# Moving the front half of a circuit layer out of the stage between attention and experts and into the attention loop

## The reference, cut to what matters

```python
x = x + cross_attention(layernorm(x), ctx, ctx)      # 32 batches, 64 queries, 1601 keys, 16 heads of 16
# the circuit layer, on y = layernorm(x):
c  = cumprod(cos(y), over the 16 columns of a head)
x1 = layernorm(y + c) * gamma1 + beta1
q  = cumprod(cos(x1[..., :16]))
f  = relu(q @ w1.T + b1) @ w2.T + b2                  # 16 -> 1024 -> 256
x  = x + layernorm(x1 + f) * gamma2 + beta2
x  = x + experts(layernorm(x))                        # shared expert + top 2 of 7
```

## Time and profile before

| what | value |
|---|---|
| time, median of 3 runs | 1946.18 us (1945.27 to 1947.3) |
| profiled execution, first to last instruction (span) | 1941.7 us |
| attention, from the first batch to the start of the last | 58 to 1388 us |
| last batch and its last weighing | 1388 to 1434 us |
| circuit layer to the first load of the experts | 1434 to 1537 us |
| experts | 1537 to 1941.7 us |

### The profile page before, as it was taken

The page is one execution under the profiler, slowest core; times in us unless marked ns, Lnnn a source line. Parts: engine busy times, 40 slices in busy tenths (PEclk is TensorE's granted clock), DMA queues, the critical chain, the costliest instruction groups (busy, mean ns, idle before and its releaser), DMA issues. The chain is left out here.

```text
span 1941.7 us, 46658 instructions
## 1 busy us (share of the span) xinstructions
PE 1876.6 (97%) x18832; PEld 1777.8 (92%) x18832; DVE 1468.1 (76%) x2796; ACT 1136.1 (59%) x1921; POOL 652.9 (34%) x643
## 2 busy tenths in 40 slices
PE   7899999999999999999999999999879889999998
PEld 5899999999999999999999999999867789999998
DVE  6777778777777777777777778777788567766667
ACT  2465666666566656666665566656765436665552
POOL 3222223322222323222223232223031126888860
PEclk9899999999999999999999999999989799999999
DMA  8666666666666666666666666667510236666633
GB/s 272 170 155 162 156 174 169 164 157 159 161 153 167 170 167 167 157 158 157 159 167 164 170 165 162 156 163 189 149 60 23 76 118 209 225 220 218 229 115 132
DMA packets 146790, 313.85 MB, mean 162 GB/s; under 512 B 57888, under 2 KB 77216, under 8 KB 143120
## 3 DMA queue, kind: packets, MB, share of 16 engines
q1 hardware_dynamic: 140672, 295.03, 56.2%
q0 software_dynamic: 4752, 13.38, 2.3%
q10 hardware_dynamic: 1152, 2.47, 0.5%
HBM read 134.20 MB, written 18.35 MB: 79 GB/s over the span
## 5 line engine op out<-in xcount | busy, mean ns | idle before, releaser
L453 ACT COPY a_pT<-a_pst 128x512 f32<-128x512 f32 x768 | 421.2, 583 | 409.0 <-PE a_pst L963 409.0
L459 ACT ACTIVATE a_probs<-a_probs,a_nmax 128x1601 f32<-128x1601 f32 x256 | 418.8, 1636 | 140.0 <-DVE a_probs L636 139.8
L636 DVE TENSOR_SCALAR_CACHE_REDUCE a_probs<-a_pss 128x1608 f32<-128x1608 f32 x256 | 467.3, 1825 | 12.8 <-PE a_pss L952 12.3
L963 PE MATMUL a_pst<-a_id,a_probs 128*128 128x128 f32 (+1 forms) x3328 | 452.6, 275 | 13.7 <-ACT a_pT L453 11.5
L963 PEld LDWEIGHTS a_pst<-a_id,a_probs 128*128 128x128 f32 (+1 forms) x3328 | 382.8, 141 | 51.1 <-issue 21.0
L355 POOL TENSOR_TENSOR a_tick<-a_tick 128x1 f32<-128x1 f32 x62 | 12.0, 193 | 953.4 <-DMA a_raw<-in_ctxT 892.1
L654 DVE TENSOR_SCALAR a_khi<-a_psk,a_bk 128x402 fp32r<-128x402 f32 x250 | 158.5, 634 | 142.9 <-PE a_psk L917 141.3
L360 POOL TENSOR_TENSOR a_clo<-a_raw,a_chi 128x402 fp32r<-128x402 f32 x240 | 247.0, 1060 | 4.8
L952 PE MATMUL a_pss<-a_kst,a_bd 96*128 96x402 f32 x1024 | 240.7, 357 | 6.4 <-DVE a_v L661 5.6
L915 PE MATMUL a_pso<-a_whi,a_chi 128*128 128x256 f32 (+1 forms) x806 | 241.9, 300 | 0.0
L917 PE MATMUL a_pso<-a_whi,a_clo 128*128 128x256 f32 (+1 forms) x806 | 227.2, 282 | 0.0
(11 more groups left out here) (251 smaller groups left out, 3511.7 us busy)
## 6 DMA issues: line engine op xcount, KB each, us to landing
a_kst<-a_khi SPq DMA_DIRECT2D x1008, 100.5 KB, 2.6
a_kst<-a_klo SPq DMA_DIRECT2D x504, 100.5 KB, 2.6
a_raw<-in_ctxT SPq DMA_DIRECT2D x60, 804.0 KB, 5.5
f_gur<-in_wgu SPq DMA_DIRECT2D x24, 1408.0 KB, 6.2
f_dr<-in_wd SPq DMA_DIRECT2D x24, 768.0 KB, 7.2
a_bd<-q_scr SPq DMA_DIRECT2D x192, 32.0 KB, 2.0
e_big<-ys_scr SPq DMA_DIRECT2D x8, 512.0 KB, 6.7
a_pT<-in_ctxT SPq DMA_DIRECT2D x2, 1608.0 KB, 9.3
```

What stands on the lines that cost most here:

```text
L453: nc.scalar.copy(pT[:, p % HALF, 4 * i:4 * i + 4, :], ps_t[:, i % 2, :].rearrange("p (t q) -> p t q", q=P)).then_inc(t_copied_act, 1)
L459: nc.scalar.activation(pr, pr, ACT.Exp, bias=nmax[:, b, p:p + 1], scale=-1.0, accum_out=esum[:, b, p:p + 1]).then_inc(probs_ready, 1)
L636: nc.vector.tensor_scalar(probs[:, p % 2, :].rearrange("p (b k) -> p b k", b=QK), ps_s[:, :, 0:KQ], -SCALE, None, ALU.mult, ALU.min, accum ...
L963: mm = nc.tensor.transpose(ps_t[0:r, i % 2, (t % 4) * P:(t % 4 + 1) * P], probs[:, p % 2, t * P:t * P + r], a_id_sb[:])
```

## The change

The front half of the circuit layer is done for each row tile inside the attention loop. For tile `it - 1`, in the batch with b = 0 and behind the two context splits, GpSimd takes the norm's power, the angle in turns, and the cosine as a polynomial (`row_cosines`, `cosines`: 18 instructions, of which 14 are 128x256). In the batch with b = 1, DVE makes the running product, the sum and the row statistics (`cumulate`, four instructions, behind the last copy of p = 2), and GpSimd centres the rows (`centre_rows`). SP stores them to a new scratch `a_scr`. Tile 15 goes the same way after attention. ACT's angles, sines and centring 1 are gone, and DVE's rounding. The second cosine is done by GpSimd for tiles 0 to 14 in one piece (`q_cosines(0)`) in the last batch and for tile 15 alone later. Groups are now five ((0,4), (4,4), (8,4), (12,2), (14,2)), the order lists are new, `idle_work` is gone, and contraction is ordered row tile by row tile.

The context is split in place: `raw` lies where `c_lo` lies, with room for both halves, so SP issues both loads together.

```diff
+            def cosines(width):
+
+                u, r, w, g = (z[:, 0:width] for z in (turn, left, square, cosine))
+                v(nc.gpsimd.tensor_scalar(w, u, ROUND, None, ALU.add))
+                v(nc.gpsimd.tensor_scalar(w, w, ROUND, None, ALU.subtract))
+                v(nc.gpsimd.tensor_tensor(out=r, in0=u, in1=w, op=ALU.subtract))
+                v(nc.gpsimd.tensor_tensor(out=w, in0=r, in1=r, op=ALU.mult))
+                v(nc.gpsimd.tensor_scalar(g, w, HALF_SINE[4], HALF_SINE[3], ALU.mult, ALU.add))
+                for k in (2, 1, 0):
+                    v(nc.gpsimd.tensor_tensor(out=g, in0=g, in1=w, op=ALU.mult))
+                    v(nc.gpsimd.tensor_scalar(g, g, HALF_SINE[k], None, ALU.add))
+                v(nc.gpsimd.tensor_tensor(out=g, in0=g, in1=g, op=ALU.mult))
+                v(nc.gpsimd.tensor_tensor(out=g, in0=g, in1=w, op=ALU.mult))
+                v(nc.gpsimd.tensor_scalar(g, g, -2.0, 1.0, ALU.mult, ALU.add))
+                v(nc.gpsimd.tensor_copy(by_head(heads[:, 0:width])[:, :, 0], by_head(g)[:, :, 0]))
+                nc.gpsimd.memset(by_head(g)[:, :, 0], 0.0).then_inc(cos_ready, 1)
...
+            def batches(it, first, last):
                 for b in range(2):
                     n = 2 * it + b
...
+                    if b == 0 and not first:
+                        row_cosines(it - 1)
...
+                    if b == 1 and not first:
+                        centre_rows(it - 1)
...
+            def cumulate(i):
+
+                dve.wait_ge(cos_ready, i + 1 if i < NT - 1 else NT + 1)
+                nc.vector.tensor_tensor_scan(left[:], cosine[:], heads[:], 0.0, ALU.mult, ALU.add).then_inc(scanned, 1)
+                dve.wait_ge(scanned, 3 * i + 1)
+                nc.vector.scalar_tensor_tensor(out=square[:], in0=turn[:], scalar=2.0 * np.pi, in1=left[:], op0=ALU.mult, op1=ALU.add).then_inc(scanned, 1)
+                dve.wait_ge(scanned, 3 * i + 2)
+                nc.vector.bn_stats(out=row_stats[:], in_=square[:]).then_inc(scanned, 1)
+                dve.wait_ge(scanned, 3 * i + 3)
+                nc.vector.bn_aggr(out=x1_mv2[:, i, :], in_=row_stats[:]).then_inc(cumulated, 1)
...
-                        if n == B - 1 and p in TURNS_IN:
...
-                                round_turns(i)
-                                leave_turns(i)
+                        if b == 1 and p == 2 and not first:
+                            cumulate(it - 1)
...
-            "turn_last.0 turn_end.0 weigh.0 project.0 turn_q.0 expand.0 expand.1 expand.2 expand.3 expand.4 expand.5 expand.6 expand.7 contract.0 turn_q.1 expand.8 "
...
+            "turn_q.0 turn_last.0 expand.0 expand.1 turn_end.0 expand.2 expand.3 weigh.0 expand.4 expand.5 expand.6 expand.7 project.0 turn_q.1 contract.0 expand.8 "
```

More of the change, by code:

```diff
@@ L300, in batches @@
                     if not last:
-                        if not (first and b == 0):
-                            sp.wait_ge(ctx_split, NC * (n + 1))
-                        load_ctx(n + 2, 0)
+                        sp.wait_ge(kv_filled, STEPS * (n + 1))
+                        for k in range(NC):
+                            load_ctx(n + 2, k)
+                    if b == 0 and it > 1:
+                        sp.wait_ge(a_ready, it - 1)
+                        sp.dma_start(a_scr[it - 2], cosine[:]).then_inc(a_stored, 16)
@@ L313, in batches @@
+                        sp.wait_ge(turn_taken, NT - 1)
+                        sp.dma_start(x_t[:], x[NT - 1]).then_inc(x_loaded, 16)
+                        for dst, src in ((row[:], rows[:, 1:]), (id_sb[:], ident), (b1_sb[:], b1), (wr_sb[:], wr), (rb_sb[:], rb)):
                             sp.dma_start(dst, src).then_inc(loaded, 16)
[L314 to L316 removed]
@@ L320, in batches @@
                         stack_keys(n + 1, 0, 0)
-                    if not last:
-                        sp.wait_ge(ctx_split, NC * (n + 1) + 1)
-                        load_ctx(n + 2, 1)
-                    if ahead:
                         stack_keys(n + 1, 0, 1)
@@ L434, in _ @@
-            pool.wait_ge(zeroed, W1_ZERO)
-            nc.gpsimd.tensor_copy(w1_sb[0:3 * HD, :], w1_raw).then_inc(w1_split, 1)
-            pool.wait_ge(w1_split, 1)
-            nc.gpsimd.tensor_tensor(out=w1_sb[2 * HD:3 * HD, :], in0=w1_raw[2 * HD:, :], in1=w1_sb[2 * HD:3 * HD, :].bitcast(F32), op=ALU.subtract).then_inc(w1_split, 1)
-            pool.wait_ge(w1_split, 2)
+                    if not last:
+                        pool.wait_ge(kv_filled, STEPS * (n + 1))
+                        for k in range(NC):
+                            pool.wait_ge(ctx_loaded[k], 16 * (n + 1))
+                            split_ctx(n + 2, b, k, raw[:, b, k])
@@ L439, in _ @@
+                    if b == 1 and not first:
+                        centre_rows(it - 1)
+            for it in range(NT):
+                batches(it, it == 0, it == NT - 1)
+            q_cosines(0)
             pool.wait_ge(expo_set, 2)
             for stage, g in POOL_ORDER:
-                if stage == "by":
-                    angles_by(1, slice(NT - 2, NT))
-                    continue
-                n = int(stage[-1])
-                pool.wait_ge(var_done[n], g + 1)
-                nc.gpsimd.tensor_tensor(out=rstd[:, tiles(g)], in0=vare[:, tiles(g)], in1=expo[:, tiles(g)], op=ALU.pow).then_inc(rstd_done[n], 1)
+                if stage == "cosines":
+                    pool.wait_ge(q_ready, 1)
+                    row_cosines(g)
+                elif stage == "centre":
+                    centre_rows(g)
+                elif stage == "turns_q":
+                    q_cosines(g)
+                else:
+                    n = int(stage[-1])
+                    pool.wait_ge(var_done[n], g + 1)
+                    nc.gpsimd.tensor_tensor(out=rstd[:, tiles(g)], in0=vare[:, tiles(g)], in1=expo[:, tiles(g)], op=ALU.pow).then_inc(rstd_done[n], 1)
@@ L540, in batches @@
                             copy_tiles(g - 1, (p - 1) % PAIRS, 2)
-                        if n == B - 2 and p in ANGLES_IN:
-                            angles(ANGLES_IN.index(p))
             for it in range(NT):
                 batches(it, it == 0)
-            act.wait_ge(expo_set, 1)
-            act.wait_ge(kv_filled, STEPS * B)
             def centre(g, n, out, src):
                 act.wait_ge(scale_set[n], g + 1)
-                if n == 1 and sum(GROUPS[g]) > NT // 2:
-                    act.wait_ge(w1_split, 2)
-                cols = slice(HD if n == 1 and g < Q_FIRST else 0, D)
                 for i in each(g):
-                    last = nc.scalar.activation(out[:, i, cols], src[:, i, cols], ACT.Identity, bias=shift[:, i:i + 1], scale=rstd[:, i:i + 1])
+                    last = nc.scalar.activation(out[:, i, :], src[:, i, :], ACT.Identity, bias=shift[:, i:i + 1], scale=rstd[:, i:i + 1])
                 last.then_inc(centred[n], 1)
             for stage, g in ACT_ORDER:
-                f = lambda z: flat(z, g)
-                if stage == "table":
-                    nc.scalar.activation(first_sin[:], x1_ex[:, 0:1], ACT.Sin)
-                elif stage == "copies":
+                if stage == "copies":
                     for i in range(2):
@@ L1098, in _ @@
                 batches(it, it == 0, it == NT - 1)
-            def idle_work(n):
-                for _ in range(n):
-                    nc.tensor.matmul(ps_f[:, 1, 0:D], id_sb[:], w2_sb[:, 0, :], start=True, stop=True)
             for stage, g in PE_ORDER:
@@ L1123, in _ @@
                         pe.wait_ge(loaded, 16 * 7)
-                    pe.wait_ge(q_ready, g + 1)
+                    pe.wait_ge(q_ready, 1 if sum(GROUPS[g]) < NT else 2)
                     if g > 0:
```

335 lines of the change are left out of this document (146 added, 189 removed), and 25 rows, old and new, of tables (ACT_ORDER, DVE_ORDER, PE_ORDER).

## The result

The changed kernel takes **1986.69 us** (median of 4 runs, 1979.44 to 1994.08), the kernel before on the same chip 1946.18. The ratio is 1.0212 (95% interval 1.0182 to 1.0242): slower by 2.1%. Forecast were 1953.3 us and a range of 1938 to 1972. The side was right, the size too small by a factor of nearly six. The runs of the changed kernel spread over 15 us, those of the one before over 2 (over 11, 1940.43 to 1951.6, in the 19 runs beside e5 to e8). The profiled run is the slowest of the four, 1994.08 us with a span of 1992.2, so +50.5 us against the span before.

What follows compares the result with a forecast made beforehand. PE was taken to bound attention and mostly the rest. Terms +13.3 - 5.8 - 1.4 + 1.0 = +7.1 us on a span of 1941.7 gave 1948.8, with 4.5 around it 1953.3 us; range 1938 to 1972.

Steps and rivals of the forecast that it cites:

- What bounds the kernel: Attention: PE is busy for 1327.73 of 1330 us, so any wait given to it there adds to the time.
- the context in place: Both context loads together, key copies queued behind: cost 0 (0 to 0.5 us a batch, up to 15).
- The rival of the collision: Attention, b = 1: DVE's sum waits for GpSimd's split copy, 1.5 us in each of 14 batches, +21, 1974 us; chance 15%.
- The four instructions: DVE's row-tile work behind pair 2, b = 1: delays PE 0.95 us a tile, +13.3 us (8 to 25).
- GpSimd in attention: A row tile's cosine on GpSimd: some 11.5 us (9 to 15) within some 32 us available, cost 0.
- The handover: Last weighing to first contraction: gain 5.6 us behind the weighing, together -5.8 us, if GpSimd's second cosine is ready.
- The contractions: Circuit stage on PE, from the first contraction on: 78 us against 79.2, so -1.4 us (-8 to +4).
- the end: Behind the contractions, one group's normalisation left on DVE: 14.2 us become some 15.2, +1.0 us (0 to +4).
- Around the span: Time outside the profiled span: 4.5 us added, as the earlier median of 1946.2 stands that far above its span.

Runs made afterwards that it cites:

- e5: On e4, GpSimd makes the second cosine of 15 tiles ahead of the first weight's split, the two weights having their own semaphore: 1942.58 us.
- e8: On e1, the row statistics (last two of DVE's four instructions) stand behind pair 5, not pair 2: 1960.54 us.
- e1: On the changed kernel, the second half of the context is loaded behind the first 12 key copies, without waiting for the split: 1955.63 us.
- e9: The kernel before with only the context split in place and both halves loaded together ahead of the key copies: 1972.48 us.
- e3: On the changed kernel, GpSimd waits in batches with b = 1 for the row tile's sums before it splits the context: 1969.76 us.
- e2: On the changed kernel, DVE's four instructions of a row tile stand at pair 0 of b = 1, not behind pair 2: 1963.05 us.
- e4: On the changed kernel, the edits of e1 and e2 together: 1942.15 us.
- e7: On e5, PE's first next-layer transposes stand behind contraction 9, and five one-operation GpSimd instructions also multiply by 1.0: 1934.63 us.

## Why the prediction was wrong

**What bounds the kernel** was read rightly: PE bounds attention, and every wait given to it there went into the time. That is why the errors are so large.

**The step that failed** is the sentence on the context in place: "The key copies queue behind the larger load; they feed DVE at pair 4, just ahead of the weighing, where DVE catches up. I cost it at 0." I named the queue and the engine, and put the price at nothing with no number for how late the copies would be. It is the largest single part of the loss: put right, it gives back 31 us with what hangs on it (e1), and alone on the kernel before it costs 29 (e9). In the profiled run the late copies themselves are 17 us of it (12.9 + 4.7 in the table, less 0.4 that the kernel before has too); the collisions, 18.6 us there (e3), come with it for the most part. DVE does catch up at a weighing, but only by as much as it would wait there (2.0 us at most in the changed kernel); the key copies were up to 3.3 late, and a copy that the weighing itself needs stands behind them (PE's 1.45 us at 885.25). In two of the half batches of the changed kernel that this lengthened, PE's clock fell behind the wait as well. The bound that I gave, up to 15 us, was too low as well: each batch can lose over 3 us, and there are 31.

**The rival of the collision** (15%) was right in its mechanism and too low in its chance. I wrote that the product would end at 717.14 and the split come at 717.07 or 717.20; rows that meet within 0.1 us say that both will happen. They met in 8 of 14 batches. I priced it at 1.5 us each, and it was 18.6 / 8 = 2.3: 1.1 to 1.4 in the three where PE's clock stayed up, 2.6 in three where it fell as well (below), 3.6 and 4.0 in two where the copy held up the product too and the clock fell. e1 adds a condition that I did not see: with the second load behind the key copies the same four instructions, at the same place, met the split in 1 batch of 14.

**The four instructions** cost 1.06 us a row tile (forecast 0.95), 14.8 us in all (forecast 13.3), 0.6 of each as a wait of PE ahead of step 7. Of DVE's 1.83 us, 0.77 cost nothing (forecast 0.8 of slack and 0.2 of wait). This term alone gave the forecast its side, and it is about a third of the loss. e1, where little else costs in attention, takes 1955.6 us, against the 1953.3 of my sum; that they are so near is in part luck, for beside its own runs of the kernel before e1 is 11.6 us slower, not 7.1, and in its profiled run the contractions took 3.8 us more and the experts 3.7 less than before. For 256 elements the product takes 0.68 (0.69) and the sum 0.42 (0.42).

**GpSimd in attention** costs nothing by its own time, as forecast, where the sums stand at pair 2. Its chain takes 14.3 us in the changed kernel (886.75 to 901.0), not 11.5 but within my 9 to 15, for the five instructions with one operation take 0.85 us and not 0.35 to 0.56. At pair 0 with both loads together (e2) it costs nothing either. With the loads apart the second split comes later, and the cosine behind it: it ends 23.1 us behind the scale's transpose at pair 4 (median of 14, e4) where it ended at 19.2 (e2, and the changed kernel). With the sums at pair 0 that leaves no margin: in e4 to e7 DVE waits for it in two to five batches, and b = 1, pair 0 to 4, has 2.1 to 5.9 us of excess in the profiled runs. So the repair of the key copies and the earlier place of the sums work against each other there.

**The handover**: behind the last weighing -6.0 us (forecast -5.6). But the condition that I had set, that GpSimd has the cosine ready, was not met: DVE waited 1.6 us for it, and the last batch came out at +4.0, where I had -0.2. With the cosine ready (e5) the last batch takes 45.4 us in the profiled run, which is -0.2, though PE still waits 2.4 us for DVE. **The contractions** came out at +1.9 (forecast -1.4), **the end** at +2.4 (+1.0): PE waits 4.6 us there for ACT's centred rows of the thirteenth and fourteenth tile. **Around the span** I took 4.5 us; the profiled run shows 1.9. The profiled run of the kernel before would have taken 1943.6 by the same 1.9, so the other 2.6 was its distance from the median of the runs. **The experts** are 1.7 to 4.6 us shorter in the profiled runs of all kernels built on the change, and 1.4 in e9 (403.1 against 404.5); I did not forecast it and have not found its cause.

**Why the parts don't add.** e9 alone costs 29 us, the four instructions 15, the collisions 19: more than the 40 that the change costs. A delay of PE at step 7 gives the key copies behind it time (e2: 4.7 became 12.2 when it went). The other way round, with the second load right behind the first, GpSimd's copy starts 1.1 us sooner after the issue, in among the four instructions (e1: 8 collisions became 1).

## What to carry to other kernels

Where a change puts a transfer ahead of others in a queue, find who waits for the *last* of those behind it and how much of an idle stretch that engine has there; "it catches up" needs a number. Rows on two engines that meet within a few tenths of a microsecond are no rival but a part of the forecast, with the share of cases in which they meet. And where one engine is busy all the time, place new work of its feeders by their waits: the same four instructions cost 1.06 us at pair 2, and nothing at pair 0, where DVE waits for the weighing, as long as what they read was ready (e2; not always in e4 to e7).

## What was unexpected in the hardware

GpSimd's tensor_scalar on 128x256 took 0.85 us with an addition alone and 0.41 with a multiplication by 1.0 behind it (e5 against e7). With a subtraction it was the other way round: 0.86 alone, 1.08 with the multiplication. Why was not tried.

The same wait of PE has two prices. In the changed kernel PE waited 1.90 us ahead of step 7 at 743.45, at 924.56 and at 1284.14 (and once more, at 1102.01), each time behind a collision. The windows from about there on (granted clock is the third figure from the right):

```profile
743.00:746.50 3.50, 3.06 (x14) 2.94 (x15) 3.35 (x8) 2.01 (x3) 3.42 (x5) 0.61 0.66 161
924.50:928.00 3.50, 3.44 (x15) 3.32 (x16) 3.05 (x8) 1.63 (x3) 3.42 (x4) 0.53 0.57 135
...
1284.00:1287.50 3.50, 3.31 (x22) 2.99 (x23) 3.43 (x8) 2.69 (x5) 3.42 (x4) 1.00 0.40 95
```

In the first two the clock is mostly at the lower of its two levels (1.2 of 2.4 GHz) and the half batch grew by 3.7 us; in the third it stays at the upper one and the half batch grew by 2.3. So it is in all eight collisions: five with a granted clock of 0.53 to 0.85 in the stretch around or behind the wait and 3.7 to 5.1 us, three with 1.00 and 2.2 to 2.4 us. At the same wait of 1.90 us the fall of the clock was worth 1.3 us; in the two half batches that grew by 4.7 and 5.1 us the wait was longer too (2.66 and 2.52). It needs no collision: behind the wait of 1.45 us at 885.25, at the weighing, the clock fell as well, and that half batch grew by 3.2 us.

```profile
887.00:890.50 3.50, 3.50 (x20) 3.50 (x19) 2.20 (x4) 2.65 (x3) 3.08 (x5) 0.52 0.54 139
```

What decides whether it falls was not tried.
